# Sums of squares accumulated by ScalarE while it squares, in place of VectorE's reductions, in an audio tower of 16 samples

## The reference

```python
def rmsnorm(x, scale, eps=1e-08):
    norm = jnp.sqrt(jnp.sum(x * x, axis=-1, keepdims=True)) / x.shape[-1] ** 0.5
    return scale * (x / (norm + eps))
...
q = xq @ Wq.T
k = xk @ Wk.T
v = xv_ @ Wv.T
g = jax.nn.sigmoid(xg @ Wg.T)
q = jnp.exp(rmsnorm(q, rms_scale))
k = jnp.exp(rmsnorm(k, rms_scale))
```

## Time and profile before

| what | value |
|---|---|
| median of 3 runs | 1056.63 us (1055.34 to 1058.45) |
| the profiled execution | 1056.37 us, span 1054.6 us |
| PE busy | 995.8 us, 94% of the span |
| DVE busy | 854.4 us, 81% |
| ACT busy | 655.9 us, 62% |
| POOL busy | 343.3 us, 33% |
| mean granted clock of TensorE | 0.986 |

### The profile page before, as it was taken

The page is one execution under the profiler, slowest core; times in us unless marked ns, Lnnn a source line. Parts: engine busy times, 40 slices in busy tenths (PEclk is TensorE's granted clock), DMA queues, the critical chain, the costliest instruction groups (busy, mean ns, idle before and its releaser), DMA issues.

```text
span 1054.6 us, 48874 instructions
## 1 busy us (share of the span) xinstructions
PE 995.8 (94%) x20963; PEld 752.3 (71%) x20963; DVE 854.4 (81%) x2690; ACT 655.9 (62%) x1240; POOL 343.3 (33%) x175
## 2 busy tenths in 40 slices
PE   5579999999999999999999999997999999999987
PEld 5467776777767677777777767776677767777754
DVE  6889888888978888897888889787698888889632
ACT  3247575756757576675667657565675757667553
POOL 5142434233233424323242423334223342423220
PEclk9879999999999999999999999999999999999999
DMA  5542415242332414333251423324233251423400
GB/s 164 153 127 71 117 48 139 63 120 65 100 89 71 124 57 122 88 93 95 72 124 56 127 85 86 102 71 111 64 93 95 71 131 50 123 70 87 110 30 19
DMA packets 71638, 97.06 MB, mean 92 GB/s; under 512 B 11360, under 2 KB 46720, under 8 KB 71424
## 3 DMA queue, kind: packets, MB, share of 16 engines
q1 hardware_dynamic: 71424, 93.94, 32.1%
HBM read 27.89 MB, written 10.83 MB: 37 GB/s over the span
## 4 chain that ended last, share of the span: by engine, by line
PE 92%; issue 3%; DVE 2%; ACT 1%; DMA 1%; POOL 0%; SPq 0%; DVEq 0%; POOLq 0%
PE bank L1004 14%; PE bank L1148 11%; PE bank L1170 11%; PE bank L1009 10%; PE bank L1141 10%; PE bank L1176 10%; PE bank L1086 7%; PE bank L1081 4%; PE bank L1118 3%; PE bank L1125 2%; PE bank L1164 2%; PE bank L1035 2%; PE bank L1076 2%; PE bank L1058 2%; PE bank L1048 1%
## 5 line engine op out<-in xcount | busy, mean ns | idle before, releaser
L605 ACT ACTIVATE hid<-bank,f1b 128x512 f32<-128x512 f32 (+1 forms) x128 | 81.8, 652 | 146.5 <-PE bank L1170 146.1
L452 POOL TENSOR_TENSOR t_sum<-x,hs 128x512 f32<-128x512 f32 x32 | 40.8, 1273 | 370.8 <-DVE x L832 276.3
L1086 PE MATMUL bank<-qx,ki 128*32 128x16 f32 x7680 | 127.2, 192 | 7.6 <-issue 7.6
L456 POOL TENSOR_TENSOR rr<-vv,nhalf 128x8 f32<-128x8 f32 x32 | 78.5, 2454 | 151.4 <-DVE vv L713 151.4
L1148 PEld LDWEIGHTS bank<-w,hid 128*128 128x128 f32 x1024 | 118.0, 192 | 8.7 <-issue 7.2
L1170 PE MATMUL bank<-xa,f1w 128*128 128x512 f32 (+1 forms) x256 | 119.6, 582 | 1.0 <-issue 0.9
L1148 PE MATMUL bank<-w,hid 128*128 128x128 f32 x1024 | 119.6, 275 | 0.8 <-ACT hid L585 0.8
L441 POOL TENSOR_TENSOR ab<-af,heads 128x1792 f32<-128x1792 f32 x16 | 78.7, 4917 | 121.6 <-DVE af L813 121.6
L1141 PE MATMUL bank<-c,w 128*128 128x512 f32 (+1 forms) x256 | 117.0, 570 | 0.9 <-ACT c L579 0.9
L1086 PEld LDWEIGHTS bank<-qx,ki 128*32 128x32 f32 x7680 | 111.5, 110 | 8.5 <-issue 8.4
L1176 PE MATMUL bank<-hid,f2w 128*128 128x512 f32 (+1 forms) x256 | 107.5, 563 | 0.0
(11 more groups left out here) (143 smaller groups left out, 2307.9 us busy)
## 6 DMA issues: line engine op xcount, KB each, us to landing
qx<-qq SPq DMA_DIRECT2D x256, 80.0 KB, 4.2
hs<-hs SPq DMA_DIRECT2D x32, 532.0 KB, 7.6
zq<-rz_dram SPq DMA_DIRECT2D x64, 128.0 KB
gz<-gate_f SPq DMA_DIRECT2D x16, 512.0 KB, 3.0
xT<-in_xT SPq DMA_DIRECT2D x16, 468.5 KB, 3.5
v_a<-v_f SPq DMA_DIRECT2D x16, 256.0 KB, 3.2
v_b<-v_f SPq DMA_DIRECT2D x16, 256.0 KB, 4.4
f1w<-in_fc1T SPq DMA_DIRECT2D x16, 256.0 KB, 2.8
```

The source lines that it names most:

```text
L456: gp.tensor_tensor(rr3[:, four(g), :], vv3[:, four(g), :], nhalf[:, 0:8].rearrange("p (m o) -> p m o", o=2), ALU.pow).then_inc(r3_ok, 1)
L605: nc.scalar.activation(hid[:, j, cols(g)], bk(f"f1_{g}{j}")[:, 0:width[g]], ACT.Gelu, bias=f1b[:, b % E, j:j + 1]).then_inc(ge2, 1)
L1086: return mm(D[r, :, t + j:t + WIN:EIGHT], ki[:, j, s0:s0 + WIN], x[:, :, t0 + j:t0 + WIN:EIGHT], start=True, stop=True)
```

## The change

ACT's squaring instruction of a bank (128x512) becomes four, one for each tile of 128x128, and each also writes the sum of its results over the columns into one column of `ssq`. The last of the four raises the semaphore on which POOL's power waits. DVE's function `sums` and its four calls per round go, with the two semaphores between ACT and DVE. ACT waits, before it squares, until POOL has taken the power of the sample before, as `ssq` is now written by ACT. The squares are still written to `qtok` and `ktok`.

```diff
@@ squares (ACT)
                 before(act, (qT_ok, kT_ok)[i], b, 2, 2)
+                before(act, rr_ok[i], b, 1, 1)
                 if i == 1:
                     before(act, kt_ok, b, 1, 1)
-                nc.scalar.activation(qk[i][:, four(g), :], by_tile(bk(f"{name}{g}")[:, :]), ACT.Square).then_inc((sq_ok, sk_ok)[i], 1)
+                src = by_tile(bk(f"{name}{g}")[:, :])
+                for j, m in enumerate(tiles(g)):
+                    last = nc.scalar.activation(qk[i][:, m, :], src[:, j, :], ACT.Square, accum_out=ssq[:, i, m:m + 1])
+                last.then_inc((rq_sum, rk_sum)[i], 1)
@@ DVE
-            def sums(b, i, g):
-                dve.wait_ge((sq_ok, sk_ok)[i], nth(b, 2, g + 1))
-                V.tensor_reduce(ssq[:, i, four(g)], qk[i][:, four(g), :], AXIS.X, ALU.add).then_inc((rq_sum, rk_sum)[i], 1)
-
@@ body (DVE)
-                if (b := at(1)) is not None:
-                    sums(b, 0, 0); sums(b, 0, 1)
                 if (b := at(2)) is not None:
                     merge(b, 5); offset2(b, 0)
                 if (b := at(1)) is not None:
-                    sums(b, 1, 0); sums(b, 1, 1); norms(b, 0); tokens(b, 0, 0); mixes(b, 3); norms(b, 1); tokens(b, 1, 0)
+                    norms(b, 0); tokens(b, 0, 0); mixes(b, 3); norms(b, 1); tokens(b, 1, 0)
                     tokens(b, 1, 1)
```

More of the change, by code:

```diff
@@ L171, in program @@
         f2_ok = sem("f2_ok"); oT_ok = sem("oT_ok")
-        h_cp = sem("h_cp"); hl_ok = sem("hl_ok"); sq_ok = sem("sq_ok"); sk_ok = sem("sk_ok")
+        h_cp = sem("h_cp"); hl_ok = sem("hl_ok");
         v_ok = sem("v_ok"); th_ok = sem("th_ok"); eq = sem("eq"); ek = sem("ek"); kt_ok = sem("kt_ok")
```

## The result

The changed kernel took 1061.49 us (median of 12 runs, 1058.55 to 1068.52) beside 1057.74 us of the kernel before: a ratio of 1.0051, 95% interval 1.0031 to 1.0071. So it is slower, by 3.3 to 7.5 us, where I had forecast 37 us. Executions recorded as slow (one of 5456 us in e11, one of 1148 us of the kernel before beside e9 to e11) are left out of all medians and ratios. The profiled execution took 1064.01 us with a span of 1062.2 us.

What follows compares the result with a forecast made beforehand. PE's in-order instruction list was taken to bound the kernel. Full rounds 32.1, round 2 3.2 and round 1 2.1 us made 37.4, added to 1056.4 for 1094 us; range 1055 to 1136.

Steps and rivals of the forecast that it cites:

- D = 4G - 3.79: PE's wait at `n2Ts` per full round, G being ACT's time for four tiles' squares: 2.29 us at G of 1.52.
- 4G - 2.34: How much later ACT's `normed2` starts in a full round, G being the time for four tiles' squares, before subtracting slack.
- The price a: Start-to-start time of one accumulated 128x128 square on ACT: taken as 0.38 us, bounds 0.18 and 0.54.
- bound from below: Lowest time per accumulated square on ACT, if the accumulator costs nothing: 0.279 - 0.10 = 0.18 us.
- The slack: How early `normed2` is ready before PE loads the first `n2Ts` weights in a full round: 1.45 us.
- Round 2: Round without expert work on PE, which already waits for `normed2`: 3.2 us lost, with no slack.
- the fall of the clock: Second rival: nothing overlaps and PE's stall in each full round also lowers its clock; 1135 to 1159 us, chance 0.12.
- G = 0.72: Lower bound for four tiles' squares on ACT: no stall in full rounds, +0.3 us in round 2, total 1056 us.
- The first rival: On ACT the accumulator's write hides behind the next squares, slack swallows it, PE never waits: 1056 us, chance 0.14.
- rival B: Follow-up theory, without a chance: loss spread over full rounds, in oftener PE pauses; 1.005 or more for the repeated changed kernel.

Runs made afterwards that it cites:

- e11: The changed kernel, unchanged, timed and profiled a second time: 1063.90 us, ratio 1.0077 to the kernel before.
- e9: Against the changed kernel, only key squares accumulate their sums on ScalarE, query squares go the old way with DVE's sums: 1059.36 us, ratio 1.0026 to the kernel before.
- e4: Kernel before with DVE's sums taken out and a constant in their place, one square per bank: 1053.55 us, ratio 0.9978.
- e6: Changed kernel plus one dead ScalarE instruction of 128x1024 before the last group of key squares, samples 2 to 15: 1075.74 us, ratio 1.0185 to the kernel before.
- e7: Changed kernel plus four dead ScalarE instructions before the last group of key squares, samples 2 to 15: 1119.13 us, ratio 1.0600 to the kernel before.
- e3: Kernel before with each bank's square split into four of 128x128 without accumulator output, DVE's sums kept: 1055.80 us, ratio 1.0009.
- e1: Changed kernel with samples 0 and 1 (rounds 1 and 2) as in the kernel before: 1058.86 us, ratio 1.0038 to the kernel before.
- e8: Changed kernel with only sample 1, squared in round 2, done as in the kernel before: 1059.92 us, ratio 1.0047 to the kernel before.
- e2: Kernel before with accumulated sums on ScalarE for samples 0 and 1 only: 1060.71 us, ratio 1.0036.

## Why the prediction was wrong

**What bounds the kernel, and where the change would be felt: right.** PE's list sets the pace, the sums on DVE were worth nothing in a full round (e4), and the place is `n2Ts`, reached over ACT's `normed2`. Made longer, ACT's list made PE wait at exactly this place, one for one (e6 and e7). The line D = 4G - 3.79 has the right slope, and its lateness is right too: 4G - 2.34 with the measured G of 1.00 is 1.66 us, measured 4.27 - 2.65 = 1.62.

**The price a: the step that failed.** I took 0.38 us per tile, with the argument that the accumulator's write "must come after the squares that it reads have ended, so it doesn't overlap them". It does overlap them in the profile's rows: the read starts 0.16 us after its square, whose row lasts 0.27 to 0.40 us, and the next square 0.09 us later. The measured a is 0.25 us, 0.16 for the square (e3) and 0.09 for the read. My own bound from below, 0.18, was 0.07 off; I moved away from it by a duration where only the distance of starts counts. The line is steep here: 14 rounds x 16 tiles make 224 times any error in a, and 0.13 x 224 is 29 of the 33 us by which I missed. With a = 0.25 the same sum gives 14 x 0.21 + 1.1 + 0.0 = 4 us, or 1060.4 us beside the measured 1061.49. That it comes so near is partly luck: its full rounds are dearer than the rows show and its round 2 cheaper, as the next paragraphs tell.

The estimate of 0.20 us per tile from the Trainium skill, page "ScalarE: Activation LUTs", section "What ACT_TABLE_LOAD costs", has no accumulator in it; the 0.16 of the split run is below that, the 0.25 with the read above. What the Trainium skill's page "VectorE: DVE Perf Modes" says of VectorE in the section "Two Vector instructions with no wait between them", an operation and then a read of the accumulator, is what the rows show on ScalarE: 256 squares and 256 reads.

**The slack: 0.2 us too small.** I counted to the first weight load of `n2Ts`, which ran 0.36 us ahead of its product. That lead was slack as well, so a full round lost 0.05 us in this stretch instead of the 0.21 of the formula.

**Round 2: the place right, the slack misread, the clock left out.** PE waited 1.03 us more, where the formula gives 1.1 at the measured a. But I had read the wait of before as one for `normed2`, with no slack. Its row names DVE's scaled queries, and with the sums left out (e4) the wait is 1.17 us instead of 1.36, and then for ACT: `normed2` had some 0.2 us of slack there too. I had named the fall of the clock only for long stalls in every round; here it came once behind 2.30 us and added 1.45 us. In the lower bound, the 0.3 us for round 2 at G = 0.72 should be 0.0 by the same formula.

**The first rival** put its point of decision at 0.24 us per tile and its time at 1056; the chip landed at 0.25, on that point, so the outcome lies between this rival and the forecast. I gave it 0.14, and it was nearer than my likeliest case. The range held the time, as it reached from one bound of a to the other, and the sign was right. The time also lies in the forecast's own range (1060 to 1120), at its lower end, but the stall of PE at `n2Ts` in every full round, which the forecast named, is not in the profile.

**What stays open.** The rows account for 1.0 to 2.5 us in round 2 and for 0.7 us in the stretch that I measured in the full rounds. Over whole full rounds it is more: PE's pauses and the time lost at the lower clock taken off, the rounds from 3 on, to the `zq` products of round 16, take 820.4 to 820.6 us in the two profiles of the changed kernel, e1 and e8, and 819.1 and 819.2 in the two of before, some 1.3 us. Together that is 2.3 to 3.8 us. The first timing says 3.3 to 7.5 us and the second 4.5 to 11.7 us. So up to several microseconds are measured and not found, some of them even at the low end of the second timing. They are of the size by which the kernel before differed from itself (0.998). The one known source of that, PE's pauses, was no larger in the changed kernel's two profiles than in the first of before. Over the six profiles with all sums of samples 2 to 15 on ScalarE the pauses add up to 19.9 to 23.8 us, 21.7 in the mean, and over the five with none of them there to 12.8 to 22.9 us, 19.0 in the mean. That leans to rival B, but the two overlap, so it is not shown that these pauses are the cause. No version that keeps the sums came out faster than the kernel before: the change loads an engine whose slack in front of PE it uses up, and frees one for which PE does not wait in a full round.

## What to carry to other kernels

Price an added chain of instructions by the distance of their starts, not by the durations of their rows, and where only durations are known give the lower part of the range its weight: here the bounds were 0.18 and 0.54 us and 0.25 was measured, and the middle of the two, 0.36, would have been hardly better than my 0.38. Multiply it by the number of instructions first: where a slack is to hold 16 of them in each of 14 rounds, a tenth of a microsecond decides between nothing and 22 us. And look at the rounds of the fill by themselves, as a slack that holds in 14 full rounds can be nearly missing in the one where a stage has no other work.

## What the runs showed of the hardware

A sum accumulated by ScalarE is an instruction of its own in the profile, a read of 128x1, and adds 0.09 us to a square of 128x128 that takes 0.16 us in a row of such. Rows of ACT grow longer while its list runs without a break (the squares from 0.27 to 0.40 us within one round, at a constant distance of 0.25 us of their starts), so mean durations overstate the price. Behind waits of PE of 1.85 to 2.9 us its granted clock was 0.50 to 0.62 in the mean over some 3 to 4 us in 13 cases (ten full rounds and round 2 of e7, round 2 of the changed kernel and of e9), at about 1.5 us each, and stayed at 1.00 in seven of the same length (four rounds of e7, round 2 of e2, of e6 and of the second execution of the changed kernel). PE's pauses for which no other engine is named stood, all 229 of more than 0.4 us, at the boundary of a block of 256 of its instructions, 1.2 to 1.8 us behind the landing of a 16 KB packet of the instruction queue; from round 3 to round 16 such pauses add up to 13 to 24 us of an execution.
